# Mamba scan with a mixture-of-experts branch: halo columns through a side buffer, and other slot tables

## Chip, cores and metric

One NeuronCore of one Trainium2 chip. The metric is the device time of one execution in microseconds (us), lower is better; the time before is the median of three executions.

## What is computed

`x` is (2, 2048, 256). It is normalised over its last axis (`xn`), and the output is `x + mamba(xn) + moe(xn)`. Cut to what matters:

```python
x_in, z = split(xn @ W_in)                       # 512 channels each
u = silu(causal_conv4(x_in) + conv_b)            # 4 taps along the time axis
dt, B, C = split(u @ W_xproj)                    # 16 + 16 + 16
delta = softplus(dt @ W_dt + b_dt)
h_t = exp(delta_t * A) * h_{t-1} + delta_t * u_t * B_t    # 16 states per channel
y_t = sum_n h_t[n] * C_t[n];   mamba = ((y + D_skip * u) * silu(z)) @ W_out
# moe: router softmax, top 2 of 16 experts, each: W1 -> layernorm -> exact gelu -> W2
```

## The kernel before

The 4096 rows are cut into 8 chunks (`NC`) of 512 time steps (`T`), four chunks to a sequence (`CPB`). In a chunk there are 4 channel blocks (`DC`) times 16 states (`NS`) = 64 **units**, numbered g = 0 to 511 over the kernel; a unit's number inside its chunk is its **slot**. The work of one unit:

- ScalarE (ACT), `exp_unit(g)`: `hb = exp(delta * A)`, into a ring of 12 rows (`HR`). ACT issues it six units (`LEAD`) ahead of its own slot, and it waits until the product of unit g-12 with C has read the ring row.
- VectorE (DVE): `product(g)` makes `psB = B * du`, `scan(g)` runs the recurrence over 512 steps in place in `hb`.
- The product with C is made for two units at once, by GpSimd (POOL) in `unit_pair(g)`; the pairs listed in `HC_DVE` are made by DVE in `times_c(g)` instead, right behind the pair's second scan. Either waits on `s_tr >= g + 2 - GR` (`GR` = 6): TensorE must have summed unit g-5, since the result goes into a ring of six rows.
- TensorE (PE), `sum_unit(g)`: four transposing matmuls add the product into `psY`, four units (`LAG`) behind PE's own slot.

Every engine walks through the 512 slots in program order, and nothing synchronises the slots of two engines but the semaphores. All other work is hung into slots by the tables `AT` (chunks 1 to 6), `AT0` (chunk 0), `AT7` (chunk 7) and, for the 20 expert groups that start at the units `GS`, `MOE` (offsets from the start). The names that matter here:

- `x_mm`, `x_in`, `x_copy`, `x_silu`: for the next chunk, project a channel block (2 matmuls), copy it from PSUM into a row of the ring `ux` (6 rows of 3 halo columns and 512 steps), convolve it (4 matmuls of the shifted row), copy back, silu. Each waits for the one before. In `x_in` ACT copies the block, and then copies its last three columns straight from PSUM into the halo columns of the row that the chunk after will use.
- `xd_mm`, `xd_copy`, `d_mm`, `d_exp`, `d_ln`, `d_max`: the projection to dt, B and C, and softplus, which ends in DVE's `d_max` (L1377). All of it goes through the one bank `psA`, so `x_mm` of the next chunk waits for the fourth `d_max` of the present one.
- `du` (POOL), `du_copy` (DVE): delta times u; `dskip` (PE): the D_skip term, first into `psY`.
- `z_mm`, `z_copy`, `z_silu`, `gate`: the gate branch. `gate(c, dc)` (DVE, L1571) waits until PE has summed the 16 units of its channel block. `gate`'s fourth entry is run in the chunk after.
- `e_tr`, `e_mm`, `e_trc`, `e_copy`: output projection of the chunk before, through bank `psC`.
- `MOE`: `load`/`load1`/`load2` are SP's loads, `t1` transposes rows on PE, `t1c` copies them on ACT (L845), `w1`, `hn`, `t2`, `t2c`, `gelu`, `w2`, `yo`, `put` follow. Banks `psC` are taken in turns (`C_TURN`), in the order in which ACT evicts them.

On DVE, slots are taken two by two: two products, two scans, then `times_c`, then all `d_max` and `gate` work of both slots. Moving an entry from slot 4 to 5, or from 3 to 2, leaves DVE's order as it was; moving one from 37 to 38 puts it one pair later. In one slot PE does `dskip`, then `sum_unit`, then the rest.

The last state of each unit is carried over a chunk boundary by ACT's `carries` (slot given by `carry`, modulo 4). Routing (16 zero rows and 64 row scatters by POOL's indirect DMAs) ends in the first 90 units.

Of the kernel before, what the change touches and what calls it, by code (L numbers as in the profile page):

```python
# [42 lines left out]
INIT_AT = 58  # L43
ETAB_AT = 40
# [35 lines left out]
    "x_load": [33],  # L80
    "x_mm": [7, 8, 10, 11, 12, 13, 18, 21, 22, 22, 23, 23, 27, 32, 32, 32, 32, 34, 34, 34, 35, 35, 37, 37],
    "x_in": [10, 19, 30, 34],
    "x_copy": [12, 22, 32],
# [18 lines left out]
AT7 = {
    "d_mm": [37, 45, 47, 3],
    "d_exp": [42, 52, 59, 4],
    "d_ln": [34, 35, 52, 6],
    "d_max": [46, 56, 61, 7],
    "du": [62, 9, 20, 36],
    "z_mm": [9, 19, 24, 29],
    "z_copy": [15, 24, 26],
    "z_silu": [32],  # L110
    "gate": [37, 42, 55, 3],
    "dskip": [0, 11, 34, 44],
    "carry": [0],
    "p_tr": [53, 56, 59, 61],
    "p_trc": [56, 58, 59, 62],
    "p_mm": [56, 58, 59, 61],
    "p_copy": [58, 58, 61, 62],
}
# [1516 lines left out]
```

## Time and profile before

| | us |
|---|---|
| three executions | 1137.55, 1130.39, 1132.38 |
| median | 1132.38 |
| the profiled execution | 1137.55 |
| its span, first to last instruction | 1135.8 |
| first scan starts | 70.1 |
| last scan ends | 1119.3 |

So the eight chunks take 1049.2 us of the span; what lies ahead is normalisation, routing and the first chunk's input, and what lies behind is the last output projection. A row of the timeline reads: start, length, engine, line, operation, output<-input, shape, count, and in brackets the idle time before it with what ended it. Merged rows overlap by some hundredths, since an instruction is started before the one ahead has drained.

### The profile page before, as it was taken

The page shows a single profiled execution, that of the slowest core. Times are in us where ns is not written, and L with a number is a line of the kernel's source. Part 1 is how long each engine was busy: PE and PEld are TensorE (multiplying, and loading weights), DVE is VectorE, ACT ScalarE, POOL GpSimd, SP SyncE. Part 2 cuts the span into 40 slices and gives each one's busy share as a digit, 9 for nine tenths or more (in the row PEclk, how much of TensorE's full clock was granted, in tenths as well). Part 3 has the DMA queues.
Part 4 walks back from the last instruction along what each step waited for, and adds up shares of the span by engine and source line. Part 5 has one row for each costly group of instructions (what it writes and reads, how often), then busy time and mean ns, then how long its engine had stood idle before and what let it go on. Part 6 is the DMA issues. An engine that isn't in the chain of part 4 may idle for free.

```text
span 1135.8 us, 16904 instructions
## 1 busy us (share of the span) xinstructions
PE 940.2 (83%) x4570; PEld 639.2 (56%) x4571; DVE 1045.8 (92%) x1308; ACT 864.9 (76%) x1839; POOL 871.0 (77%) x562
## 2 busy tenths in 40 slices
PE   4927776497998999779998999899988999887865
PEld 3414343363566656556666766576656666666544
DVE  7887999999999988968998989999999999999894
ACT  4544698556698799857999689978998799976971
POOL 5057899699778788756878767977987887887894
PEclk9957887589889999879997999899997999889989
DMA  9576457973376424825447652873457543855313
GB/s 305 188 271 241 137 183 225 316 291 83 112 245 204 107 69 122 312 82 112 103 104 233 210 107 67 255 235 57 107 151 249 133 116 87 291 169 108 70 19 65
DMA packets 119367, 185.86 MB, mean 164 GB/s; under 512 B 12012, under 2 KB 104344, under 8 KB 111016
## 3 DMA queue, kind: packets, MB, share of 16 engines
q1 hardware_dynamic: 87120, 144.60, 37.7%
q0 software_dynamic: 19584, 25.26, 13.0%
q10 hardware_dynamic: 12568, 14.93, 4.3%
q8 instruction: 36, 0.59, 0.2%
q14 instruction: 59, 0.48, 0.1%
HBM read 146.34 MB, written 42.60 MB: 166 GB/s over the span
## 4 chain that ended last, share of the span: by engine, by line
PE 36%; DVE 18%; issue 16%; ACT 14%; POOL 9%; DMA 4%; ACTq 2%; SPq 1%; POOLq 0%; DVEq 0%
DVE hb L1555 10%; PE psY L1087 8%; POOL hc L624 5%; PE psA L1112 4%; PE psC L1225 4%; PE psA L1160 3%; ACT hb L798 3%; PE psE L1202 3%; PE psC L1175 3%; PE psA L1104 2%; DVE psB L1544 2%; ACT hnT L913 2%; PE psA L1148 2%; DMA xg<-xs_d 1%; POOL xs_d L638 1%
## 5 line engine op out<-in xcount | busy, mean ns | idle before, releaser
L624 POOL TENSOR_TENSOR hc<-hb,Cb 128x1024 f32<-128x1024 f32 x245 | 621.2, 2640 | 108.2 <-PE psY L1087 65.4
L1555 DVE TENSOR_TENSOR_SCAN hb<-hb,carry,psB 128x512 f32<-128x512 f32 x384 | 470.9, 1261 | 6.8 <-ACT hb L798 5.0
L798 ACT ACTIVATE hb<-delta,aneg 128x512 f32<-128x512 f32 x512 | 351.9, 716 | 27.5 <-POOL hc L624 21.0
L1087 PE MATMUL psY<-ident,hc 128*128 128x128 f32 x2048 | 308.0, 292 | 71.1 <-POOL hc L624 70.8
L1087 PEld LDWEIGHTS psY<-ident,hc 128*128 128x128 f32 x2048 | 258.1, 151 | 183.8 <-POOL hc L624 94.1
L1544 DVE TENSOR_TENSOR psB<-Bb,psU 128x512 f32<-128x512 f32 x512 | 324.6, 678 | 3.2 <-DMA Bb<-bc_d 3.2
L672 POOL DMA_INDIRECT out<-yo,idx x80 | 128.8, 1610 | 56.8 <-DMA out<-yo,idx 16.9
L1555 DVE TENSOR_TENSOR_SCAN hb<-hb,psB 128x512 f32<-128x512 f32 x128 | 149.3, 1202 | 0.0
L1112 PE MATMUL psA<-ux,dgw 128*128 128x512 f32 x232 | 114.0, 607 | 1.6 <-ACT ux L739 1.4
L1225 PE MATMUL psC<-w2r,hnT 128*128 128x256 f32 x320 | 89.8, 429 | 0.0
L631 POOL TENSOR_TENSOR du<-delta,ux 128x512 f32<-128x512 f32 x32 | 47.2, 1474 | 53.9 <-DVE delta L1377 51.8
L1202 PE MATMUL psE<-w1r,xgT 128*128 128x256 f32 x320 | 85.0, 411 | 0.0
L1225 PEld LDWEIGHTS psC<-w2r,hnT 128*128 128x128 f32 x320 | 63.9, 210 | 18.8 <-issue 10.4
L1202 PEld LDWEIGHTS psE<-w1r,xgT 128*128 128x128 f32 x320 | 60.9, 200 | 17.5 <-issue 10.1
L1104 PE MATMUL psA<-xnT,win 128*128 128x512 f32 x116 | 59.2, 629 | 11.7 <-ACT zs L822 7.8
L1160 PE MATMUL psA<-win,xnT 128*128 128x512 f32 x128 | 63.8, 623 | 1.1 <-ACT ux L745 1.1
L913 ACT ACTIVATE hnT<-hnT,vecs 128x128 f32<-128x128 f32 x160 | 63.8, 480 | 0.3
L1175 PE MATMUL psC<-wout,ygT 128*128 128x256 f32 x248 | 61.0, 389 | 1.3 <-ACT ygT L831 1.2
L1148 PE MATMUL psA<-xr,rows 16*128 16x512 f32 x60 | 42.0, 786 | 20.3 <-DVE delta L1377 19.6
L1112 PEld LDWEIGHTS psA<-ux,dgw 128*128 128x128 f32 x232 | 40.9, 196 | 27.3 <-issue 23.4
L1175 PEld LDWEIGHTS psC<-wout,ygT 128*128 128x128 f32 x248 | 45.9, 196 | 7.4 <-ACT ygT L831 2.0
L638 POOL DMA_INDIRECT xs_d<-xg,slots x37 | 39.2, 1059 | 14.2 <-issue 7.0
(233 smaller groups left out, 1198.2 us busy)
## 6 DMA issues: line engine op xcount, KB each, us to landing
Bb<-bc_d SPq DMA_DIRECT2D x32, 1024.0 KB, 7.1
Cb<-bc_d SPq DMA_DIRECT2D x32, 1024.0 KB, 7.4
w1r<-w1c_d SPq DMA_DIRECT2D x80, 256.0 KB
w2r<-in_L_ffn_W SPq DMA_DIRECT2D x80, 256.0 KB, 3.4
xg<-xs_d SPq DMA_DIRECT2D x20, 516.0 KB
xg<-xn_d SPq DMA_DIRECT2D x37, 128.0 KB, 2.8
Bb<-in_L_attn_x SPq DMA_DIRECT2D x8, 512.0 KB, 8.2
xn_d<-hb SPq DMA_DIRECT2D x8, 512.0 KB, 7.9
```

What stands on the lines that cost most here:

```text
L624: pool.tensor_tensor(hc[:, k:k + 2, :], hb[:, g % HR:g % HR + 2, :], Cb[:, n:n + 2, :], ALU.mult).then_inc(s_g, 1)
L672: pool.indirect_dma_start(out=out[:, :], out_offset=bass.IndirectOffsetOnAxis(ap=idx[:, g % 2, j:j + 1], axis=0), in_=yo[:, j, :], in_offs ...
L798: act.activation(hb[:, g % HR, :], delta[:, dc, :], ACT.Exp, scale=aneg[:, dc, n:n + 1]).then_inc(s_exp, 1)
L913: ins = act.activation(hnT[:, j, kc, :], hnT[:, j, kc, :], ACT.Gelu, scale=g1t[:, bass.ds(e, 1), kc], bias=be1t[:, bass.ds(e, 1), kc])
L1087: mm = pe.matmul(y[:, tt * P:(tt + 1) * P], hc[:, g % GR, tt * P:(tt + 1) * P], ident[:, :], start=False, stop=(n == NS - 1), is_transpose ...
L1112: mm = pe.matmul(bank[:, :], dgw[:, dc, k, :], x_of(p, dc)[:, k:k + T], start=(k == 0), stop=(k == KW - 1))
L1160: mm = pe.matmul(psA[:, :], xnT[:, c % 2, kc, tt * P:(tt + 1) * P], win[:, 1, kc, :], start=(kc == 0), stop=(kc == KC - 1))
L1175: mm = pe.matmul(psC[:, 0:D], ygT[:, dc, :], wout[:, dc, :], start=(dc == 0), stop=(dc == dc_out(c) - 1))
L1202: mm = pe.matmul(psE[:, a * D:(a + 1) * D], xgT[:, a, kc, :], w1r[:, a, kc, :], start=False, stop=(kc == KC - 1), skip_group_check=True)
L1225: mm = pe.matmul(psC[:, a * D:(a + 1) * D], hnT[:, 2 * h + a, kc, :], w2r[:, 2 * h + a, kc, :], start=False, stop=(kc == KC - 1), skip_gro ...
L1544: dve.tensor_tensor(psB[g % 2][:, :], Bb[:, n, :], psU[:, :], ALU.mult).then_inc(s_dbu, 1)
L1555: dve.tensor_tensor_scan(h, h, psB[g % 2][:, :], first, ALU.mult, ALU.add).then_inc(s_scan, 1)
```

## The change

The halo of a channel block no longer goes from PSUM into the row of the next chunk. `x_in` now makes three copies, in this order: the row's own halo columns (from zeros at the start of a sequence, else from a new side buffer `halo` that the chunk before filled), the last three columns of the PSUM bank into `halo`, and the block itself. All three count on `s_xi`, which the convolution waits for. With that, a `memset` of `ux` on DVE and PE's wait for DVE's constants at its start are gone. The last chunk makes the three copies too, where it made one.

The other part is in the tables. One `HC_DVE` list takes the place of another: pairs 180, 204, 274 and 416 go to POOL, pairs 22, 64, 72, 78 and 142 come to DVE. `AT`, `AT0`, `AT7`, `MOE`, `CEN0`, `INIT_AT` and `ETAB_AT` have entries moved by one to seven slots.

```diff
-INIT_AT = 58
-ETAB_AT = 40
+INIT_AT = 53
+ETAB_AT = 42
...
 AT = {
-    "x_load": [36],
+    "x_load": [33],
-    "xd_copy": [46],
-    "d_mm": [50, 55, 58, 3],
+    "xd_copy": [47],
+    "d_mm": [50, 55, 57, 3],
-    "d_max": [55, 58, 62, 4],
-    "du": [53, 0, 25, 26],
+    "d_max": [55, 58, 62, 5],
+    "du": [53, 4, 24, 29],
-    "gate": [30, 45, 54, 3],
+    "gate": [30, 45, 52, 2],
...
 AT0 = {
-    "d_mm": [46, 50, 59, 6],
+    "d_mm": [47, 51, 59, 4],
...
-    "d_max": [50, 58, 62, 18],
-    "d0_exp": [4, 6, 6],
-    "d0_max": [7, 8, 8],
+    "d_max": [51, 59, 60, 15],
+    "d0_exp": [2, 3, 5],
+    "d0_max": [5, 7, 9],
...
-    "gate": [33, 41, 52, 27],
+    "gate": [31, 43, 50, 25],
...
-    "carry": [1],
+    "carry": [0],
...
 AT7 = {
-    "z_silu": [32],
-    "gate": [37, 42, 55, 3],
+    "z_silu": [33],
+    "gate": [38, 41, 55, 3],
...
-HC_DVE = [2, 10, 12, 20, 54, 56, 86, 180, 204, 274, 416]
+HC_DVE = [2, 10, 12, 20, 22, 54, 56, 64, 72, 78, 86, 142]
...
 MOE = {
-    "load": [0],
-    "load1": [0, 3],
+    "load": [1],
+    "load1": [1, 4],
-    "t1": [2, 13],
+    "t1": [3, 13],
-    "idx": [6],
+    "idx": [9],
-    "t2c": [14, 22],
+    "t2c": [13, 22],
...
-CEN0 = 19
+CEN0 = 21
...
+        halo = sb("halo", [P, 2, DC, HALO])
...
                 act.wait_ge(s_du, j - UR + 1)
+                if p == 0:
+                    act.wait_ge(s_cdve, NCONST)
+                elif p % CPB:
+                    act.wait_ge(s_xi, 3 * (j - DC) + 2)
+                act.activation(x_of(p, dc)[:, 0:HALO], halo0[:, :] if p % CPB == 0 else halo[:, (p - 1) % 2, dc, :], ACT.Copy).then_inc(s_xi, 1)
+                act.activation(halo[:, p % 2, dc, :], bank[:, T - HALO:T], ACT.Copy).then_inc(s_xi, 1)
                 act.activation(u_of(p, dc), bank[:, :], ACT.Copy).then_inc(s_xi, 1)
-                if p + 1 < NC:
-                    if j + DC >= UR:
-                        act.wait_ge(s_xp, j + DC - UR + 1)
-                    if p == 0:
-                        act.wait_ge(s_cdve, NCONST)
-                    act.activation(x_of(p + 1, dc)[:, 0:HALO], halo0[:, :] if (p + 1) % CPB == 0 else bank[:, T - HALO:T],
-                                   ACT.Copy).then_inc(s_xi, 1)
...
-                    pe.wait_ge(s_xi, 2 * (p * DC + dc + 1) if p + 1 < NC else 2 * p * DC + dc + 1)
+                    pe.wait_ge(s_xi, 3 * (p * DC + dc + 1))
...
             pe.wait_ge(s_const, 2)
-            pe.wait_ge(s_cdve, NCONST)
...
-            dve.memset(ux[:, 0:DC, 0:HALO], 0.0).then_inc(s_cdve, 1)
```

## Rows read from the trace of the kernel before

**Rows 1.** The page's first two parts: busy time, and TensorE's granted clock.

```profile
PE 940.2 (83%) x4570; PEld 639.2 (56%) x4571; DVE 1045.8 (92%) x1308; ACT 864.9 (76%) x1839; POOL 871.0 (77%) x562
...
PEclk9957887589889999879997999899997999889989
```

**Rows 2.** Busy time in windows, slots 1 to 45 of chunks 1, 3, 5, then clock, DMA.

```profile
233.50:321.30 87.80, 76.18 (x351) 48.30 (x350) 87.77 (x100) 56.98 (x122) 75.14 (x47) 0.94 0.48 149
...
489.10:587.40 98.30, 91.15 (x426) 60.52 (x425) 84.52 (x98) 77.97 (x151) 67.88 (x45) 0.96 0.35 80
...
754.20:842.10 87.90, 85.51 (x420) 57.52 (x419) 86.47 (x101) 76.99 (x161) 72.56 (x44) 1.00 0.47 117
```

**Rows 3.** Groups of instructions by shape: DVE's pairs, POOL's pairs, the halo copy.

```profile
L624 POOL TENSOR_TENSOR hc<-hb,Cb 128x1024 f32<-128x1024 f32 x245 | 621.2, 2640 | 108.2 <-PE psY L1087 65.4 <-DVE hb L1555 39.7 <-ACT yo L926 1.3
...
L1564 DVE TENSOR_TENSOR hc<-hb,Cb 128x1024 f32<-128x1024 f32 x11 | 20.0, 1821 | 22.6 <-PE psY L1087 22.4
...
L739 ACT ACTIVATE ux<-psA 128x3 f32<-128x3 f32 x21 | 3.6, 170 | 0.0
```

**Rows 4.** DVE's timeline at the four pairs that leave it: 180, 204, 274, 416.

```profile
454.17 1.23 DVE L1564 TENSOR_TENSOR hc<-hb,Cb 128x1024 f32<-128x1024 f32 x1 [3.57 <-PE psY L1087]
...
515.99 1.22 DVE L1564 TENSOR_TENSOR hc<-hb,Cb 128x1024 f32<-128x1024 f32 x1 [12.74 <-PE psY L1087]
...
658.31 1.22 DVE L1564 TENSOR_TENSOR hc<-hb,Cb 128x1024 f32<-128x1024 f32 x1 [3.89 <-PE psY L1087]
...
933.25 3.14 DVE L1564 TENSOR_TENSOR hc<-hb,Cb 128x1024 f32<-128x1024 f32 x1
```

**Rows 5.** ACT's and DVE's timelines at unit 228, at unit 302, at unit 430.

```profile
556.58 1.94 ACT L798 ACTIVATE hb<-delta,aneg 128x512 f32<-128x512 f32 x3
...
559.00 1.26 DVE L1544 TENSOR_TENSOR psB<-Bb,psU 128x512 f32<-128x512 f32 x2
560.17 2.44 DVE L1555 TENSOR_TENSOR_SCAN hb<-hb,carry,psB 128x512 f32<-128x512 f32 x2
562.53 1.27 DVE L1544 TENSOR_TENSOR psB<-Bb,psU 128x512 f32<-128x512 f32 x2
...
706.55 0.72 ACT L798 ACTIVATE hb<-delta,aneg 128x512 f32<-128x512 f32 x1
...
707.91 1.21 DVE L1555 TENSOR_TENSOR_SCAN hb<-hb,psB 128x512 f32<-128x512 f32 x1
...
956.50 0.72 ACT L798 ACTIVATE hb<-delta,aneg 128x512 f32<-128x512 f32 x1
957.11 0.20 ACT L804 ACTIVATE carry<-hb 128x4 f32<-128x4 f32 x1
957.21 1.94 ACT L798 ACTIVATE hb<-delta,aneg 128x512 f32<-128x512 f32 x3
...
959.34 1.28 DVE L1555 TENSOR_TENSOR_SCAN hb<-hb,carry,psB 128x512 f32<-128x512 f32 x1
```

**Rows 6.** Timelines in chunk 0's first units: DVE's fourth d_max; PE; ACT.

```profile
96.37 0.75 DVE L1377 SCALAR_TENSOR_TENSOR delta<-psA,vecs,tmpA 128x512 f32<-128x512 f32 x1 [3.51 <-ACT tmpA L787]
...
89.38 2.82 PE L1087 MATMUL psY<-ident,hc 128*128 128x128 f32 x12 [24.78 <-POOL hc L624]
92.13 2.07 PE L1148 MATMUL psA<-xr,rows 16*128 16x512 f32 x2
...
94.23 0.69 ACT L780 ACTIVATE tmpA<-psA,bneg 128x512 f32<-128x512 f32 x1 [2.16 <-PE psA L1148]
```

**Rows 7.** Timelines at chunk 0's slots 50 to 52: PE, then DVE.

```profile
188.75 2.07 PE L1148 MATMUL psA<-xr,rows 16*128 16x512 f32 x2 [2.56 <-DVE delta L1377]
...
193.81 0.69 DVE L1571 TENSOR_TENSOR zs<-zs,psY 128x512 f32<-128x512 f32 x1 [1.67 <-PE psY L1087]
```

**Rows 8.** DVE's timeline at three other stalls: units 66, 150 and 486.

```profile
227.18 0.69 DVE L1571 TENSOR_TENSOR zs<-zs,psY 128x512 f32<-128x512 f32 x1 [2.65 <-PE psY L1087]
...
389.37 2.45 DVE L1555 TENSOR_TENSOR_SCAN hb<-hb,carry,psB 128x512 f32<-128x512 f32 x2 [1.74 <-ACT carry L804]
...
1070.84 0.69 DVE L1571 TENSOR_TENSOR zs<-zs,psY 128x512 f32<-128x512 f32 x1 [2.57 <-ACT zs L822]
```

**Rows 9.** Who waited for whom, whole run: us in total, times, longest us.

```profile
ACT xgT L845 <- PE psC L1184: 2.8, 5, 1.1
```

More of the change, by code:

```diff
@@ L79 @@
 AT0 = {
[L80 to L83, printed above, removed]
+    "x_load": [26],
+    "x_mm": [7, 7, 10, 11, 12, 13, 18, 21, 22, 22, 23, 23, 27, 32, 32, 32, 32, 33, 34, 34, 35, 35, 36, 36],
+    "x_in": [9, 19, 30, 34],
+    "x_copy": [13, 22, 32],
     "x_silu": [38],
-    "xd_mm": [37, 41, 43, 43],
+    "xd_mm": [38, 41, 43, 45],
     "xd_copy": [43],
-    "d_mm": [46, 50, 59, 6],
-    "d_exp": [47, 52, 59, 7],
-    "d_ln": [48, 54, 59, 9],
-    "d_max": [50, 58, 62, 18],
-    "d0_exp": [4, 6, 6],
-    "d0_max": [7, 8, 8],
-    "du": [50, 8, 21, 35],
-    "z_mm": [14, 18, 23, 26],
-    "z_copy": [17, 19, 23],
+    "d_mm": [47, 51, 59, 4],
+    "d_exp": [45, 52, 58, 5],
+    "d_ln": [49, 55, 60, 10],
+    "d_max": [51, 59, 60, 15],
+    "d0_exp": [2, 3, 5],
+    "d0_max": [5, 7, 9],
+    "du": [50, 4, 21, 30],
+    "z_mm": [14, 18, 23, 27],
+    "z_copy": [16, 18, 22],
     "z_silu": [26],
-    "gate": [33, 41, 52, 27],
-    "dskip": [3, 13, 35, 51],
-    "bc_load": [47, 57, 63, 63],
-    "carry": [1],
+    "gate": [31, 43, 50, 25],
+    "dskip": [3, 9, 36, 51],
+    "bc_load": [47, 57, 62, 62],
+    "carry": [0],
 }
 AT7 = {
[L103 to L109, printed above, removed]
-    "z_silu": [32],
-    "gate": [37, 42, 55, 3],
[L112 to L115, printed above, removed]
+    "d_mm": [44, 48, 53, 1],
+    "d_exp": [36, 51, 60, 3],
+    "d_ln": [35, 42, 59, 6],
+    "d_max": [47, 57, 62, 6],
+    "du": [62, 9, 19, 34],
+    "z_mm": [11, 21, 24, 30],
+    "z_copy": [15, 24, 27],
+    "z_silu": [33],
+    "gate": [38, 41, 55, 3],
+    "dskip": [4, 9, 35, 40],
+    "carry": [1],
+    "p_tr": [55, 57, 59, 60],
+    "p_trc": [55, 58, 59, 60],
     "p_mm": [56, 58, 59, 61],
-    "p_copy": [58, 58, 61, 62],
+    "p_copy": [57, 58, 60, 62],
 }
-HC_DVE = [2, 10, 12, 20, 54, 56, 86, 180, 204, 274, 416]
+HC_DVE = [2, 10, 12, 20, 22, 54, 56, 64, 72, 78, 86, 142]
 PUT0 = -1
@@ L424, in build @@
         NBIG = 5
-        NCONST = 7
+        NCONST = 6
         xt = x.rearrange("(g a p) d -> g p a d", p=P, a=TT)
```

## Prediction

> **What bounds the kernel now.** I read the page's busy times first. DVE is busy 92% of the span, PE 83%, POOL 77% and ACT 76% [rows 1]. That alone says that DVE is the bound, and that whatever takes work or idle time off DVE shortens the run. The windows by part of a chunk say that this is half the truth. In slots 1 to 45 of chunk 5, PE is busy 85.51 of 87.90 us at a granted clock of 1.00 while DVE is busy 86.47 of the same: both are full. In chunk 1 the same slots have DVE at 87.77 of 87.80 and PE at 76.18: DVE alone binds. In chunk 3, PE is busy 91.15 of 98.30 and DVE only 84.52: PE binds, and DVE's idle time is a symptom [rows 2]. So from chunk 2 on there are two regimes. In slots 5 to 45 PE carries the next chunk's input, the gate branch and the output projection, and ACT is tied to it, since it evicts each of these in order. From slot 46 on PE has little but sums, and DVE binds. In chunks 0 and 1 DVE binds throughout.
>
> The reader is to take one thing from this: an idle DVE microsecond is worth a microsecond only if the exponentials that its later scans read are ready that much earlier than they are used. How much earlier is read in two timelines, by the end of an exponential on ACT and the start of the scan of the same unit on DVE. I call that the slack. It is small around slot 46, right behind ACT's silu of the next chunk, because this silu stands at the end of PE's long chain.
>
> **Pairs that leave DVE.** Each of the four costs its own time and the stall in front of it, where DVE waits for PE's sum of unit g-5 [rows 4].
>
> - 204: 12.74 + 1.22 = 14.0 us of DVE. Chunk 3 is where PE binds. Unit 228's exponential, the first of three from 556.58, ends near 557.3, and its scan starts at 560.17 [rows 5]. If ACT's times stay, DVE can be 2.9 us earlier there and no more. I take 2.9; the other bound is 14.0.
> - 274: 3.89 + 1.22 = 5.1 us. Unit 302's exponential ends at 706.55 + 0.72 = 707.27, its scan starts at 707.91: slack 0.6. I take 0.6; bound 5.1.
> - 416: 3.1 us of its own, no stall. Unit 430: 957.22 against 959.34, slack 2.1. I take 2.1; bound 3.1.
> - 180: 3.57 + 1.23 = 4.8 us. It lies behind slot 46, so DVE binds. But `gate(2, 2)` moves from slot 54 to 52, and then stands right behind the scans of units 180 and 181, waiting for the sum of unit 175, which is the very sum that the pair waited for. The stall stays and has another name. I take 1.2; if PE comes earlier by itself, 4.8.
>
> Sum: 2.9 + 0.6 + 2.1 + 1.2 = 6.8 us gained, against 27.0 if DVE's time were the whole story. For POOL, which is busy 77%, these are four pairs more and five less.
>
> **Pairs that come to DVE.** The eleven of before have a mean of 1.821 us [rows 3], from 1.22 to 3.14 [rows 4]. Pair 22 stands in chunk 0 and pairs 72 and 78 in chunk 1, where nothing hides them: 3 x 1.8 = 5.4 us. Pair 64 stands just ahead of a `gate` that waits 2.65 us for PE, and pair 142 ahead of a stall of 1.74 us on ACT [rows 8]: cover enough, so nothing; without it 3.6 us. They relieve POOL in the part where it scatters the routed rows, but no scan there waits for POOL, so I give nothing for that.
>
> The 3.14 us of pair 416 ran beside a product of POOL's, the 1.22 did not. The Trainium skill (SBUF — State Buffer, section "SBUF: two separate sides") says that DVE and GpSimd share one port pair as an exclusive lock, which a DVE operation with two SBUF inputs takes part in, and that the loser blocks for the whole instruction. The trace agrees as far as it goes. By that rule a DVE pair costs 1.2 us beside an idle POOL and up to POOL's whole instruction more beside a busy one. It gives a rival below.
>
> **First units.** Of `d_max` 1 to 3 in chunk 0, the last waits 3.51 us, because `d_mm(0, 3)` stands in PE's slot 6, behind three sums (12 matmuls, 2.82 us) that begin only when POOL's first pair is ready at 89.38; its ACT work starts at 94.23 and the result is used at 96.37 [rows 6]. In slot 4 the matmul stands behind one sum instead of three, that is 2/3 x 2.82 = 1.9 us earlier, and it runs alone, not as the second of two, 1.0 us earlier by half of 2.07. `d0_exp` 2 and 3 now lie ahead of the exponential that waits for POOL, so ACT is free for it. The wait ahead of the fourth `d_max` and 0.8 us ahead of the third shrink: I take 1.9 + 1.0 + about 0.2 = 3.1 us, bounds 0 and 3.51 + 0.8 = 4.3. Afterwards DVE binds, so it stays gained.
>
> **Gate in chunk 0.** The third `gate` waits 1.67 us for PE, which itself waited 2.56 us in `d_mm(1, 1)` of slot 50 for DVE [rows 7], ahead of the sum of unit 47. The gate moves a pair earlier (559.00 to 562.53, so 3.5 us [rows 5]), which alone would cost 3.5 us more of waiting; but `d_mm` moves to slot 51, behind that sum in PE's order, and PE no longer waits there. I take 1.7 us gained; if the sum isn't ready, up to 1.7 + 3.5 lost against that.
>
> **Last chunk.** The first `gate` waits 2.57 us for ACT's z [rows 8]. It moves one pair later (two products and two scans, 3.5 us), and z one slot later (1.8 us, half a pair): 3.5 - 1.8 = 1.7, of which all is gained: 1.8 us with rounding; bounds 0 and 2.6.
>
> **Halo.** 4 blocks x 7 chunks get one small copy more, and the last chunk's 4 get two: 36. Such a copy takes 0.17 us [rows 3], but ACT starts the next instruction 0.10 us after a small one has started (957.11 and 957.21 [rows 5]), since they overlap. It lies on ACT, ahead of the convolution that PE waits for. Where ACT has no slack at slot 46, four copies cost 0.4 us; that is some chunks of 2 to 6, and elsewhere DVE hides it. I take 1.0 us lost, bounds 0 and 36 x 0.17 = 6.1. The new wait on `s_xi` is for ACT's own copies a chunk ago and holds up nothing; the one on `s_cdve` is for memsets long done, and the exponentials behind it wait for nothing new. The `memset` and PE's first wait go from a place where PE waits for the normalised rows anyway: nothing. Without that cover, one small instruction, about the 0.17 us of the small copy.
>
> **Other moves.** `d_max` 4 to 5, `gate` 3 to 2 and `du` 25 to 24 leave the order as it was. `du` 0 to 4 and 26 to 29 let POOL's pair go first and are still ahead of DVE's copy in slots 14 and 46: nothing. `xd_copy`, `x_load`, `load`, `load1`, `idx`, `CEN0`, `INIT_AT` and `ETAB_AT` move work and DMA issues that have slots to spare, past no wait that is late today; `ETAB_AT` moves DVE work inside a DVE-bound chunk. `t1` 2 to 3 is the one that I don't give away: see the third rival.
>
> **Sum.** -6.8 + 5.4 - 3.1 - 1.7 - 1.8 + 1.0 = -7.0 us. Against the profiled execution, 1137.55, that is 1130.5. This one was 5.2 us above the median of the three runs, 1132.38, so the forecast for the median is 1132.4 - 7.0 = **1125.4 us**, 0.6% faster.
>
> **Rival 1, DVE's time counts in full.** The exponentials come earlier too, because PE and ACT are not really full. For it: the Trainium skill (Perfetto Trace Analysis, section "Identifying the Most-Contended Engine") warns that the busy share of matmuls says little of how close TensorE is to its limit, and wants the busy share of weight loads, which in chunk 5's window is 57.52 of 87.90. By that page there would be a third left. Against it: PE's matmuls follow each other there without gaps, 85.51 of 87.90, and fewer microseconds need fewer or faster matmuls, which the change doesn't bring. Time: the gains for 204, 274 and 416 become 14.0, 5.1 and 3.1, so 16.6 more: 1125.4 - 16.6 = 1108.8 us.
>
> **Rival 2, nothing is left.** The new DVE pairs meet POOL, which is at its busiest in chunks 0 and 1 (75.14 of 87.80 in chunk 1's window [rows 2]), and each costs 3.1 us as pair 416 did. Pairs 22, 72, 78 cost 9.3 in place of 5.4, pairs 64 and 142 outgrow their cover by 0.5 + 1.4 = 1.9, and the halo copies cost 2.8 in place of 1.0: 7.6 more, 1133.0 us. Pair by pair it depends on where POOL stands, so I don't expect all five.
>
> **Rival 3, slower.** `t1` on PE moves from offset 2 to 3, its copy on ACT stays at 4. Where PE and ACT run level, ACT gets to the copy before PE has made the transposes, and the exponentials behind it in ACT's queue wait, and DVE's scans for them. Today this wait is 2.8 us over 5 of 40 copies [rows 9]. A PE slot is about 87.9 / 44 = 2.0 us; half a slot for each of the 20 groups is 20 us, so 1125.4 + 20 = 1145.4. It makes the run slower than before from 7.0 / 20 = 0.35 us a group, and by over 1% from 0.9. Against it: 14 of the 20 groups start outside slots 28 to 45, where there is slack of several us.
>
> **How the numbers follow.** Forecast 0.45, rival 1 0.18, rival 2 0.22, rival 3 0.15. The forecast's own range is 1118 to 1131: the bounds of the halo and of the gates on one side, half of pair 204 on the other. Over 1% faster means under 1121.1; a change of less than about 1% can hardly be told from none. All of rival 1 and 0.19 of the rest lie there: 0.37. Over 1% slower (above 1143.7) is two thirds of rival 3: 0.10. Within 1%: 0.53. The range for 8 in 10 is 1111 to 1140, which leaves out the far part of rivals 1 and 3.
>
> **What would show it.** Right: in slots 1 to 45 of chunk 3 PE is as busy as before and DVE's idle time is spread over waits for `hb`; chunk 1 is longer by 3 to 4 us; the fourth `d_max` of chunk 0 comes near 93.3; at slot 52 of chunk 2 the `gate` waits some 3.5 us for PE; the gaps of `times_c` fall from 22.6 to some 2 us. Wrong: chunk 3's window of 98.30 us falls to near chunk 5's 87.90 (rival 1); DVE pairs of 3 us (rival 2); ACT's copy L845 idle before it by 10 us or more (rival 3). The clock could undo all of it: chunk 3 starts at a low granted clock, and whether it does so again depends on when PE falls idle at the chunk's end, which I can't forecast.

## The result, and the profile after

| us | before | after |
|---|---|---|
| median (executions) | 1131.28 (7) | 1140.44 (7) |
| lowest to highest | 1126.86 to 1137.55 | 1135.98 to 1144.74 |
| the profiled execution | 1137.55 | 1138.76 |
| its span | 1135.8 | 1137.0 |

The ratio is 1.0076, with a 95% interval of 1.0048 to 1.0104: the change costs some 9 us, where 7 us less were forecast. Of 40 executions of after, 39 lie between 1133.56 and 1148.23 us, with a median of 1139.34, and one, at a mean granted clock of 0.554, took 1550.57 and is in none of the other figures. The two profiled executions differ by 1.2 us only, since that of before was one of its longest and that of after lies under its own median. A cause can therefore not be read from one pair of traces; it took kernels with one part of the change each (next section).

The busy times of after, the page's first part, then TensorE's granted clock [rows 1]:

```profile
PE 935.7 (82%) x4571; PEld 639.7 (56%) x4571; DVE 1044.7 (92%) x1308; ACT 866.9 (76%) x1875; POOL 867.4 (76%) x561
...
PEclk9967895697979999889998999899997999899887
```

PE is busy 4.5 us less than before, POOL 3.6 and DVE 1.1 us less, ACT 2.0 us more. So in these two traces no engine has more work that would pay for 9 us; what the change costs is waiting. The windows answer to [rows 2], again from the sum of slot 1 to the same sum as there, in chunks 1, 3 and 5 of after:

```profile
228.60:316.60 88.00, 77.17 (x347) 48.86 (x346) 87.90 (x101) 57.68 (x126) 69.20 (x45) 0.91 0.46 141
486.80:583.80 97.00, 89.69 (x427) 59.78 (x425) 84.57 (x98) 78.33 (x155) 69.91 (x43) 0.98 0.36 82
755.70:845.10 89.40, 85.23 (x419) 57.54 (x418) 87.55 (x102) 77.51 (x165) 73.06 (x48) 1.00 0.48 123
```

Chunk 3 went from 98.30 to 97.00 us, nowhere near chunk 5's length, and chunk 5 from 87.90 to 89.40. Chunk 1, which the new pairs 72 and 78 were to lengthen by 3 to 4 us, went from 87.80 to 88.00: they took 1.22 and 1.23 us, and pair 86 in the same window took 1.51 us where it had 3.27 before (the last section says why). The groups of after, by shape: DVE's pairs, POOL's pairs, the two halo copies, and the matmuls of `d_mm`, the last row of all being that of before, which was not shown ahead (busy us, mean ns | idle before, and what ended it):

```profile
L1562 DVE TENSOR_TENSOR hc<-hb,Cb 128x1024 f32<-128x1024 f32 x12 | 20.1, 1676 | 1.6 <-PE psY L1087 1.3
L625 POOL TENSOR_TENSOR hc<-hb,Cb 128x1024 f32<-128x1024 f32 x244 | 616.6, 2667 | 113.7 <-PE psY L1087 73.8 <-DVE hb L1553 29.9 <-ACT yo L926 4.6
L738 ACT ACTIVATE ux<-halo 128x3 f32<-128x3 f32 x32 | 6.4, 201 | 10.8 <-PE psA L1104 8.1 <-PE psC L1104 1.0 <-PE psY L1104 1.0
L739 ACT ACTIVATE halo<-psA 128x3 f32<-128x3 f32 x29 | 4.6, 160 | 0.0
L1148 PE MATMUL psA<-xr,rows 16*128 16x512 f32 x60 | 41.7, 781 | 34.8 <-DVE delta L1375 34.1 <-ACT xr L765 0.7
```

```profile
L1148 PE MATMUL psA<-xr,rows 16*128 16x512 f32 x60 | 42.0, 786 | 20.3 <-DVE delta L1377 19.6 <-ACT xr L765 0.7
```

The gaps of DVE's pairs fell from 22.6 to 1.6 us, as wanted [rows 3]. What has grown is the wait of `d_mm` for `d_max`, from 19.6 to 34.1 us.

### The profile page after: what moved, and what is told of

It is laid out like the page before. It is cut to its first block, busy times and chain, and to the rows that moved or that the text cites. A ratio compares the mean times of both kernels' runs of the same rounds, so it can differ in the third digit from the quotient of the medians.

```text
span 1137.0 us, 16966 instructions
## 1 busy us (share of the span) xinstructions
PE 935.7 (82%) x4571; PEld 639.7 (56%) x4571; DVE 1044.7 (92%) x1308; ACT 866.9 (76%) x1875; POOL 867.4 (76%) x561
## 4 chain that ended last, share of the span: by engine, by line
PE 39%; ACT 18%; issue 15%; DVE 12%; POOL 10%; ACTq 3%; DMA 2%; SPq 0%; POOLq 0%; DVEq 0%
PE psY L1087 9%; POOL hc L625 7%; DVE hb L1553 6%; ACT hb L798 5%; PE psC L1225 5%; PE psA L1112 4%; PE psC L1175 4%; PE psE L1202 3%; PE psA L1160 3%; PE psA L1104 3%; ACT hnT L913 3%; PE psA L1148 2%; POOL out L673 2%; DVE psB L1542 1%; DMA xg<-xs_d 1%
## 5 line engine op out<-in xcount | busy, mean ns | idle before, releaser
L1225 PE MATMUL psC<-w2r,hnT 128*128 128x256 f32 x320 | 89.7, 429 | 0.0
L1225 PEld LDWEIGHTS psC<-w2r,hnT 128*128 128x128 f32 x320 | 63.8, 210 | 18.5 <-issue 10.2
L1148 PE MATMUL psA<-xr,rows 16*128 16x512 f32 x60 | 41.7, 781 | 34.8 <-DVE delta L1375 34.1
L1160 PE MATMUL psA<-win,xnT 128*128 128x512 f32 x128 | 61.2, 601 | 1.5 <-ACT ux L745 1.1
L926 ACT ACTIVATE yo<-psC,wv 128x256 f32<-128x256 f32 x80 | 33.3, 469 | 27.2 <-PE psC L1225 24.2
```

Source lines behind the costliest of these rows:

```text
L1160: mm = pe.matmul(psA[:, :], xnT[:, c % 2, kc, tt * P:(tt + 1) * P], win[:, 1, kc, :], start=(kc == 0), stop=(kc == KC - 1))
L1225: mm = pe.matmul(psC[:, a * D:(a + 1) * D], hnT[:, 2 * h + a, kc, :], w2r[:, 2 * h + a, kc, :], start=False, stop=(kc == KC - 1), skip_gro ...
```

## Experiments

Each kernel is the one before with the stated edit, unless it says otherwise. Its ratio to the kernel before is from executions on the same chip, so medians of different rows are not to be compared with each other. n is the number of executions.

| kernel | edit | median (n) | ratio | 95% interval |
|---|---|---|---|---|
| list_only | all of `HC_DVE` | 1131.31 (12) | 0.9979 | 0.9959 to 0.9998 |
| list_drop | 180, 204, 274, 416 to POOL, none added | 1128.31 (12) | 0.9988 | 0.9972 to 1.0003 |
| halo_only | the halo through the side buffer | 1131.99 (12) | 0.9998 | 0.9977 to 1.0019 |
| tables_only | all of `AT`, `AT0`, `AT7`, `INIT_AT`, `ETAB_AT`, `CEN0` | 1137.82 (12) | 1.0034 | 1.0013 to 1.0056 |
| at_only | `AT` | 1136.06 (12) | 1.0030 | 1.0009 to 1.0052 |
| at0_only | `AT0`, the three constants | 1130.50 (12) | 1.0001 | 0.9980 to 1.0022 |
| at7_only | `AT7` | 1131.03 (12) | 0.9986 | 0.9969 to 1.0002 |
| moe_only | all of `MOE` | 1139.13 (6) | 1.0070 | 1.0043 to 1.0098 |
| moe_loads | `load`, `load1`, `idx` | 1138.21 (6) | 1.0070 | 1.0050 to 1.0090 |
| moe_t1 | `t1` | 1135.03 (12) | 1.0039 | 1.0020 to 1.0057 |
| moe_t2c | `t2c` | 1131.79 (12) | 1.0006 | 0.9988 to 1.0023 |
| moe_load01 | `load`, `load1` | 1132.12 (12) | 1.0016 | 0.9992 to 1.0039 |
| moe_idx | `idx` | 1137.21 (12) | 1.0060 | 1.0035 to 1.0085 |
| fill9 | four extra copies on POOL at offset 9 | 1131.41 (12) | 1.0004 | 0.9980 to 1.0027 |
| fill6 | the same at offset 6 | 1131.16 (12) | 1.0003 | 0.9984 to 1.0021 |
| after_old_moe | after, with `MOE` of before | 1137.56 (6) | 1.0053 | 1.0032 to 1.0073 |
| after_idx6 | after, with `idx` back at 6 | 1135.61 (12) | 1.0034 | 1.0016 to 1.0052 |
| best | `HC_DVE` and `AT7` | 1131.23 (12) | 0.9995 | 0.9977 to 1.0013 |

### The four parts of the change

list_only, halo_only, tables_only and moe_only each take over one part of the diff, whole. The theory was that the pairs bring back less than their slack, the rivals that a table or the halo costs.

> The kernel before with the new HC_DVE list alone. Slack theory (a DVE microsecond counts only up to the slack of the exponentials): 6.8 us gained and 5.4 us lost, so -1.4 us, ratio 0.999. Theory that DVE time counts in full: -27.0 + 5.4 = -21.6 us, ratio 0.981. Theory that the list is what made the changed kernel slower (the pairs in chunks 0 and 1 cost 3 us each or more, and POOL falls behind where it took pairs over): +5 to +10 us, ratio 1.004 to 1.009.

> The kernel before with the halo's way through the side buffer alone, all tables as before. My prediction: +1.0 us, ratio 1.001. Theory that the order of the three copies makes it slower (two small copies stand ahead of the block's own copy, so each convolution starts later, on PE's full stretch): 28 blocks times 0.2 to 0.3 us, +5.6 to +8.4 us, ratio 1.005 to 1.0075.

> The kernel before with the new AT, AT0 and AT7 and the moved constants INIT_AT, ETAB_AT, CEN0 alone, the list, MOE and the halo as before. My prediction: -3.1 -1.7 -1.8 us = -6.6 us, ratio 0.994. Rival: the gates and softplus steps moved earlier wait for what is not ready, +3 us or more, ratio 1.003 or more.

> The kernel before with the new MOE offsets alone. My prediction: 0, ratio 1.000. Third rival (the row transposes one slot later on PE, ACT waits for them ahead of its copy and the exponentials behind it are late): +5 to +20 us, ratio 1.005 to 1.018.

The list gains 0.2%, the halo is worth nothing either way, and the two parts that were costed at next to nothing cost 0.3% and 0.7%. Added up this is +0.81%, against +0.76% for the whole: the four parts account for it.

### Inside the expert table

```diff
 moe_t1:       -    "t1": [2, 13],       +    "t1": [3, 13],
 moe_t2c:      -    "t2c": [14, 22],     +    "t2c": [13, 22],
 moe_load01:   -    "load": [0], "load1": [0, 3],    +    "load": [1], "load1": [1, 4],
 moe_idx:      -    "idx": [6],          +    "idx": [9],
 moe_loads:    both of moe_load01 and moe_idx
```

> The kernel before with the first row transposes (t1) in offset 3 in place of 2, nothing else. Theory T1 (these transposes a slot later on PE are what the MOE offsets cost, since the two slots between them and the first products with W1 shrink to one and ACT's copy lies in between): most of the 0.70% of moe_only, ratio 1.004 to 1.007. Theories T2 and L below: 1.000.

> The kernel before with ACT's copy of the first half's second transposes (t2c) in offset 13 in place of 14. Theory T2 (ACT gets to the copy before PE has made the transposes, and exponentials wait behind it): ratio 1.003 to 1.007. T1 and L: 1.000.

> The kernel before with load in offset 1, load1 in 1 and 4, and idx in 9 (before: 0, 0 and 3, 6). Theory L (SP loads the routed rows later behind loads of B and C, or POOL makes the row numbers later): ratio 1.003 to 1.007. T1 and T2: 1.000.

> The kernel before with load in offset 1 and load1 in 1 and 4 (before 0, and 0 and 3), nothing else. Theory S (the routed rows and W1 are asked for behind what SP waits for in the slot between, so they land later; the groups that start at slots 56 and 57 of a chunk fall behind a load of B and C): ratio 1.004 to 1.007. Theory I: 1.000.

> The kernel before with idx (POOL's row numbers of an expert group) in offset 9 in place of 6, nothing else. Theory I (POOL is disturbed by the four small operations in their new place): ratio 1.004 to 1.007, most of the 0.70% of moe_loads. Theory S (it is SP's loads): 1.000.

`idx` alone costs 0.6%: four short instructions on POOL, three slots later. What it does is seen in the second half of chunk 4. POOL's timeline of moe_load01, where `idx` is at offset 6:

```profile
694.00 2.94 POOL L624 TENSOR_TENSOR hc<-hb,Cb 128x1024 f32<-128x1024 f32 x1
696.34 0.90 POOL L656 TENSOR_SCALAR padv<-xg,padrow 128x4 f32<-128x4 f32 x1
696.62 0.75 POOL L657 COPY wv<-xg 128x4 f32<-128x4 f32 x1
697.46 0.20 POOL L659 TENSOR_TENSOR padv<-xg,padv 128x4 f32<-128x4 f32 x1
697.72 0.19 POOL L661 CAST idx<-padv 128x4 int32<-128x4 f32 x1
702.97 2.36 POOL L624 TENSOR_TENSOR hc<-hb,Cb 128x1024 f32<-128x1024 f32 x1 [5.06 <-DVE hb L1555]
705.48 1.63 POOL L672 DMA_INDIRECT out<-yo,idx  x1 [0.15 <-issue]
706.61 2.90 POOL L624 TENSOR_TENSOR hc<-hb,Cb 128x1024 f32<-128x1024 f32 x1
709.79 1.59 POOL L672 DMA_INDIRECT out<-yo,idx  x1 [0.28 <-DMA out<-yo,idx]
```

The same of moe_idx, then its PE and its DVE:

```profile
703.05 2.37 POOL L624 TENSOR_TENSOR hc<-hb,Cb 128x1024 f32<-128x1024 f32 x1 [5.81 <-PE psY L1087]
705.58 1.58 POOL L672 DMA_INDIRECT out<-yo,idx  x1 [0.15 <-issue]
706.60 2.95 POOL L624 TENSOR_TENSOR hc<-hb,Cb 128x1024 f32<-128x1024 f32 x1
708.93 0.91 POOL L656 TENSOR_SCALAR padv<-xg,padrow 128x4 f32<-128x4 f32 x1
...
711.05 1.62 POOL L672 DMA_INDIRECT out<-yo,idx  x1 [0.54 <-PE psY L1087]
712.16 5.23 POOL L624 TENSOR_TENSOR hc<-hb,Cb 128x1024 f32<-128x1024 f32 x2
...
715.13 0.66 PE L1087 MATMUL psY<-ident,hc 128*128 128x128 f32 x4 [1.34 <-POOL hc L624]
...
723.54 0.75 DVE L1377 SCALAR_TENSOR_TENSOR delta<-psA,vecs,tmpA 128x512 f32<-128x512 f32 x1 [1.05 <-ACT tmpA L787]
```

At offset 6 the four instructions lie in a gap of POOL's that costs nothing. At offset 9 they stand between a pair and a row add in a stretch without gaps: both kernels start a pair within 0.01 us of each other (706.61 and 706.60), and the pairs after it start at 710.82 and 712.16, 1.34 us apart. PE's next sum waits the same 1.34 us, and DVE's `d_max` 1.05 us. The place decides, not the work, which is the same 1.6 us in both.

The other groups agree. In before, POOL stands idle for over 1 us right behind the four instructions in 14 of the 20 groups, 49.2 us in all; in moe_idx in 2 of 20, 8.8 us in all. Another measure is the end of each unit's scan on DVE, set against the end of the same scan in another trace. By it moe_idx loses 3.9 us on moe_load01 from unit 80 to the last. Its median is 6.7 us above before's; the trace shows less, since its profiled execution (1133.74) is 3.5 us under that median.

fill9 and fill6 ask whether POOL's time at those offsets costs by itself. They add copies that nothing reads:

```diff
+                            if off == 9:      # 6 in fill6
+                                for k in range(4):
+                                    pool.tensor_copy(fil[:, k, :], zrow[:, 0:GT])
```

> The kernel before, idx in offset 6 as it was, with four extra small POOL copies (128 x 4, zeros into a spare tile, nothing waits for them) in offset 9 of each of the 20 groups. Capacity theory (from offset 8 on POOL has a row add in nearly every pair of units, so any POOL work there delays the pairs that PE sums): about as much as moe_idx or a little more, ratio 1.004 to 1.008. Theory that idx costs through what waits for its result or through the work it waits for: 1.000 to 1.001.

> The same four extra copies in offset 6, right behind idx. Capacity theory: POOL has slack there, ratio 1.000 to 1.002. Theory that POOL is at its limit everywhere and about 1 us of POOL work costs the same in any slot: the same as fill9, 1.004 or more.

Neither costs anything that can be measured. In the group rows the 80 copies of fill9 are busy for 15.9 us, that is 0.8 us a group, those of fill6 for 10.9; the four instructions of `idx` take from 696.34 to 697.91, 1.57 us. If the cost went with POOL's time at offset 9, fill9 would cost 0.8 / 1.57 of 0.60%, which is 0.31%; its interval ends at 0.27%. But `idx`'s own interval, 0.35 to 0.85%, makes that 0.18 to 0.43%, so this doesn't hold the two apart. Excluded is a cost of 0.4% or more for 0.8 us of POOL's time at offset 9, as the capacity theory had it. Whether `idx` costs more than its time on POOL, by its chain of semaphore waits or by what waits for its result, stays open.

`t1` costs 0.39%. Rival 3 named a place for it: ACT's copy L845 waiting for PE. That wait, over the whole run, in moe_t1 and then in after (us, times, longest) [rows 9]:

```profile
ACT xgT L845 <- PE psC L1184: 3.6, 5, 1.1
...
ACT xgT L845 <- PE psC L1184: 7.0, 6, 1.9
```

In moe_t1 it is 0.8 us more than in before. So the mechanism is there, and the wait that shows isn't the price: 0.39% is 4.4 us (2.3 to 6.4), against 0.8 us of wait. The largest loss against halo_only's trace is 2.7 us at the start of chunk 4, where the last `gate` of chunk 3 waits 3.44 us for PE (0.77 in halo_only); but before's own profiled execution waits 3.71 us there. And moe_t1's profiled execution (1131.41) is 3.6 us under its median, so most of the cost may not be in this trace at all. What `t1` costs, and by what, is not settled.

### Inside the slot tables

```diff
 at_only, its core:
-    "d_mm": [50, 55, 58, 3],     "gate": [30, 45, 54, 3],
+    "d_mm": [50, 55, 57, 3],     "gate": [30, 45, 52, 2],
 at0_only, its core:
-    "d_max": [50, 58, 62, 18],   "d0_exp": [4, 6, 6],
+    "d_max": [51, 59, 60, 15],   "d0_exp": [2, 3, 5],
 at7_only, its core:
-    "z_silu": [32],              "gate": [37, 42, 55, 3],
+    "z_silu": [33],              "gate": [38, 41, 55, 3],
```

> The kernel before with the new AT alone (chunks 1 to 6: x_load, xd_copy 47, third d_mm 57, du 4, 24, 29, third gate 52). I predicted nothing for it beside the gate. Theory A (gate in slot 52 waits 3 to 4 us for PE in each of chunks 2 to 4, and xd_copy a slot later delays the softplus chain at the chunk's end): ratio 1.002 to 1.005. Theory B (AT7): 1.000.

> The kernel before with the new AT0 (chunk 0) and INIT_AT, ETAB_AT, CEN0 alone. My prediction: -3.1 -1.7 = -4.8 us, ratio 0.996. The trace of tables_only shows 3.2 us lost by the start of chunk 1 against the profiled execution before; if that is the tables' whole cost, ratio 1.003.

> The kernel before with the new AT7 (chunk 7) alone. My prediction: -1.8 us, ratio 0.998. Theory B (the later z matmuls and the earlier softplus of the last block cost at the start and middle of chunk 7): ratio 1.002 to 1.004.

`AT` is the one that costs. By the ends of its scans it falls behind halo_only mostly at the seams between chunks: by 1.9 us from unit 112 to 128, 0.6 from 176 to 192, 3.8 from 240 to 272, 0.8 from 304 to 320, 0.9 from 368 to 384. Of the 3.8, 2.7 aren't `AT`'s to pay: they are the wait of the last `gate` of chunk 3 for PE, 3.43 us here and 3.71 in before, where halo_only has 0.77. Chunk 7, which `AT` doesn't touch, differs by another 2.9. The seam at slot 57 of chunk 1 in at_only, PE's, ACT's and DVE's timelines:

```profile
330.82 1.09 PE L1087 MATMUL psY<-ident,hc 128*128 128x128 f32 x8
336.04 2.07 PE L1148 MATMUL psA<-xr,rows 16*128 16x512 f32 x2 [4.13 <-DVE delta L1377]
...
339.62 3.78 PE L1225 MATMUL psC<-w2r,hnT 128*128 128x256 f32 x8
...
343.44 0.84 ACT L926 ACTIVATE yo<-psC,wv 128x256 f32<-128x256 f32 x2 [3.14 <-PE psC L1225]
...
345.44 0.75 DVE L1377 SCALAR_TENSOR_TENSOR delta<-psA,vecs,tmpA 128x512 f32<-128x512 f32 x1 [1.77 <-ACT tmpA L787]
```

and in before, PE and DVE:

```profile
338.49 1.12 PE L1148 MATMUL psA<-xr,rows 16*128 16x512 f32 x2
...
344.94 0.72 DVE L1377 SCALAR_TENSOR_TENSOR delta<-psA,vecs,tmpA 128x512 f32<-128x512 f32 x1
```

The edit is `d_mm` 58 to 57 for the third channel block. This matmul writes `psA`, which the second `d_max` frees at DVE's slot 58. In before PE did a sum and the second half of an expert product first, and the bank was free by then. One slot earlier, PE stands for 4.13 us with this matmul at the head of its queue. All that follows is late: an expert output, for which ACT waits 3.14 us, then the softplus behind it, then DVE, 1.77 us. On top of it, the two matmuls of `d_mm` take 2.07 us after PE's idle time and the eight of L1225 3.78, where before has 1.12 and 2.27. The granted clock behind PE's busy times shows why; the first row is of at_only, the second of before:

```profile
333.14:343.38 10.24, 7.34 (x16) 4.24 (x17) 10.24 (x12) 7.03 (x18) 6.21 (x3) 0.50 0.92 314
```

```profile
330.06:336.88 6.82, 6.82 (x19) 3.81 (x18) 6.82 (x9) 6.14 (x13) 6.30 (x8) 0.50 0.86 297
```

Both fall to the lower level (1.2 GHz), before for 6.82 us, at_only for 10.24 from a moment inside the wait. After shows the same at the same place: 4.84 us of PE's wait, 1.77 us of DVE's. Over the whole run, `d_mm` waits for `d_max` 35.3 us in at_only, 21.1 in halo_only. No kernel has the one `d_mm` entry alone, so what `xd_copy`, the `du` entries and the third `gate` add to the 0.30% is not known.

`AT0` wins 1.15 us at the third `gate` of chunk 0 (0.52 us of wait against 1.67) and gives it back behind: its third `d_max`, moved from slot 62 to 60, waits 2.13 us where before has no wait, and the two waits after it are 1.28 and 1.94 us against 2.65 and 1.41, so 1.3 us more in all. At the first units it gains nothing either: the fourth `d_max` comes 24.56 us behind the first scan's start, 26.26 in before, but pair 10 behind it takes 3.96 us and not 2.42, and at unit 12 DVE is where it was. `AT7` gains 0.14%, within its interval of nothing.

### The list without its additions

```diff
-HC_DVE = [2, 10, 12, 20, 54, 56, 86, 180, 204, 274, 416]
+HC_DVE = [2, 10, 12, 20, 54, 56, 86]
```

> The kernel before with pairs 180, 204, 274 and 416 given to POOL and none given to DVE. Slack theory: 2.9 + 0.6 + 2.1 + up to 4.8 for pair 180, whose gate stays in slot 54 here, so -6.8 to -10.4 us, ratio 0.991 to 0.994. Theory that DVE time counts in full: -27.0 us, ratio 0.976. Theory that POOL is too late with four pairs more: 1.000 or more.

It gains 0.12%, about 1.4 us, where the sum had 6.8 for these four pairs. DVE's stalls in chunk 3 of list_drop, between 500 and 590 us, which are all the rows with idle time there:

```profile
508.33 1.28 DVE L1555 TENSOR_TENSOR_SCAN hb<-hb,carry,psB 128x512 f32<-128x512 f32 x1 [3.34 <-ACT hb L798]
511.02 1.28 DVE L1555 TENSOR_TENSOR_SCAN hb<-hb,carry,psB 128x512 f32<-128x512 f32 x1 [0.22 <-ACT hb L798]
512.51 1.28 DVE L1555 TENSOR_TENSOR_SCAN hb<-hb,carry,psB 128x512 f32<-128x512 f32 x1 [0.21 <-ACT hb L798]
516.68 1.28 DVE L1555 TENSOR_TENSOR_SCAN hb<-hb,carry,psB 128x512 f32<-128x512 f32 x1 [0.52 <-ACT hb L798]
521.70 2.45 DVE L1555 TENSOR_TENSOR_SCAN hb<-hb,carry,psB 128x512 f32<-128x512 f32 x2 [2.55 <-ACT hb L798]
537.70 0.69 DVE L1533 COPY psU<-du 128x512 f32<-128x512 f32 x1 [0.57 <-POOL du L631]
546.14 0.69 DVE L1571 TENSOR_TENSOR zs<-zs,psY 128x512 f32<-128x512 f32 x1 [6.57 <-ACT zs L820]
```

Together 3.34 + 0.22 + 0.21 + 0.52 + 2.55 + 0.57 + 6.57 = 13.98 us. The 12.74 us in front of pair 204 and its own 1.22 were 13.96. Before has 1.04 us of waiting for the same `gate`, so 12.9 us came back in these rows, within 40 us of time and under three other names. The rest went too: by the ends of its scans list_drop is 5.10 us ahead of before at unit 204, 18.74 at unit 206 and 5.15 at unit 224. (After and best keep 2.0 and 2.3 us of it there, list_only nothing.) The largest single wait is one that the slack didn't look at: the `gate` at slot 30 waits for ACT's z. ACT had no idle time from 534 us to this z. Before that, from 498 to 534 us, it waited for PE 13 times, 14.1 us in all, and each of these waits is within 0.02 us of the one in before: PE and ACT ran as they had, whatever DVE did.

The same reading for the other three: pair 180 leaves 1.4 us, of which half is gone at unit 198, pair 274 nothing and pair 416 1.1 us, where this kernel's sum had up to 4.8, 0.6 and 2.1.

### Do the parts add up?

```diff
 after_idx6, against after:
-    "idx": [9],
+    "idx": [6],
 best, against before (and AT7 as in at7_only):
-HC_DVE = [2, 10, 12, 20, 54, 56, 86, 180, 204, 274, 416]
+HC_DVE = [2, 10, 12, 20, 22, 54, 56, 64, 72, 78, 86, 142]
```

> The changed kernel with the MOE offsets of before. If the parts add up (list 0.9979, halo 0.9998, tables 1.0034): ratio to the kernel before 1.001, that is 1133 to 1134 us, 6 to 7 us under the changed kernel. If the MOE offsets cost only in the company of the old tables: 1.005 or more.

> The changed kernel with one entry put back: idx at offset 6 instead of 9. Theory (idx alone costs 0.6%, because POOL's four short instructions fall into a stretch where pairs and row adds follow each other without a gap): 1140.4 - 6.8 = 1133.6 us, ratio to the kernel before 1.002 (1.000 to 1.004), that is the AT part (0.3%) and t1 (0.4%) stay, the list (-0.2%) and AT7 (-0.1%) are against them. Rival (in the changed kernel the costs of idx, t1 and AT overlap, each filling slack that another has used, as the kernel with the old MOE table at 1.0053 hints): it stays at 1.005 or above, and the single costs are not a sum.

> The kernel before with only the two parts of the change that measured below 1: the new HC_DVE list (0.9979) and AT7 (0.9986). Theory: they lie in different chunks (1 to 6, and 7), so they add: ratio 0.9965, about 1127.4 us against a before of 1131.4. Rival (DVE's time won ahead of chunk 7 is given back there, since chunk 7 waits for its DMA load and for PE): 0.998 to 1.000.

The four parts do, 0.81% against 0.76%. Smaller pieces come out lower than their sums, each time by about as much as the intervals are wide. Undoing `idx` in the changed kernel takes the ratio from 1.0076 to 1.0034, 0.42% where it costs 0.60% alone; that is inside the theory's range, and the rival's 1.005 is not reached. With all of the old `MOE` it is 1.0053, where 0.9979 x 0.9998 x 1.0034 gives 1.0011: 0.42% apart, with some 0.41% of uncertainty. Inside `MOE`, the four singles sum to 1.21% against 0.70% for the table, 0.51% apart with 0.51% of uncertainty. The two gaining parts together, which should have given 0.9965, give 0.9995, 0.30% apart with 0.31%. (These uncertainties are estimates: the half widths of the intervals, squared, added and rooted.) None of the kernels is faster than before by an amount that this measurement holds apart from none, except the list, barely. That costs share a slack, so that what one edit has used the next can't use again, would explain the pattern; it is argued here, not shown.

## Why the prediction was wrong

The step that failed is the paragraph "Other moves". It costed `idx`, `AT`'s third `d_mm` (not even named there) and the slots of `AT0`'s `d_max` at nothing, by "slots to spare, past no wait that is late today". Against that stand +0.60% for `idx`, 6.8 us, and +0.30% for `AT`, 3.4 us. What the runs show in place of slots to spare: behind `idx` at offset 6 POOL has a gap in 14 of 20 groups, at offset 9 in 2; and `d_mm` a slot earlier comes ahead of the `d_max` that frees its bank, 4.13 us of wait at one seam. The second step that failed is a size, that of the pairs that leave DVE: 1.4 us for 6.8. Point by point:

- **Two regimes, PE and DVE.** Right: chunk 3's window stayed at 97.00 us with DVE's idle time spread over other waits. By rival 1 list_drop would have gained 27.0 us; it gained 1.4. The Trainium skill (Perfetto Trace Analysis, section "Identifying the Most-Contended Engine") wants the busy share of weight loads, beside the share of peak arithmetic, read in place of the busy share of matmuls. Here the trace sides with matmuls, 85.51 of 87.90 [rows 2]: the third that weight loads seem to leave was not there for this change to use.
- **Pairs that leave DVE, 6.8 us.** The mechanism was right, the size too big: 1.4 us (interval -0.3 to 3.2). The slack to the exponential of one later unit was taken, unit 228 for pair 204; that exponential is one of several ends of PE's chain, and a nearer one, the z of the `gate` at unit 222, decided. In list_only and list_drop, DVE's lead over halo_only shrinks across chunk 3 (unit 192 to 224: 3.6 to 2.0 us and 4.9 to 4.3): nothing is won there.
- **The gate at slot 52 of chunk 2** waits 4.15 us for PE, forecast "some 3.5": right. The stall kept its size and changed its name.
- **Pairs that come, 5.4 us.** The rows of after for 22, 72 and 78 are 1.22, 1.22 and 1.23 us, 3.7 in all. Pair 64 took 3.45 us, more than its cover of 2.65. Pair 142 took 1.49, and its cover, the stall of 1.74 us, is gone from after. Rival 2's 3.1 us held for one of five. As list_only (0.9979) and list_drop (0.9988) don't differ, the five together cost nothing that shows; 5.4 us, 0.48%, is outside the uncertainty of that difference, about 0.25%. (The mean of 1.8 us hid two kinds of pair, see the last section; and the longest of the eleven was pair 86 with 3.27, not 416 with 3.14.)
- **First units, 3.1 us.** Wrong, and hidden by luck. DVE is 3.3 us earlier at unit 12 in after, which looks like a hit. But the wait ahead of the fourth `d_max` was to shrink and is 3.46 us, against 3.51; the `d_max` comes at 94.70, not near 93.3. After's and at0_only's DVE, and before's pair 10:

```profile
79.56 1.29 DVE L1542 TENSOR_TENSOR psB<-Bb,psU 128x512 f32<-128x512 f32 x2 [2.41 <-DMA Bb<-bc_d]
...
94.70 0.75 DVE L1375 SCALAR_TENSOR_TENSOR delta<-psA,vecs,tmpA 128x512 f32<-128x512 f32 x1 [3.46 <-ACT tmpA L787]
...
100.14 1.23 DVE L1562 TENSOR_TENSOR hc<-hb,Cb 128x1024 f32<-128x1024 f32 x1 [1.25 <-PE psY L1087]
```

```profile
101.27 3.96 DVE L1564 TENSOR_TENSOR hc<-hb,Cb 128x1024 f32<-128x1024 f32 x1 [1.87 <-PE psY L1087]
```

```profile
102.26 2.42 DVE L1564 TENSOR_TENSOR hc<-hb,Cb 128x1024 f32<-128x1024 f32 x1 [1.70 <-PE psY L1087]
```

  Of the 3.3 us, 0.7 come from a load of B that DVE waited 2.41 and not 3.16 us for, about 1.0 from the third `d_max`, whose wait of 0.82 us is gone, and 1.6 from pair 10 and the wait ahead of it. With the same `AT0`, at0_only has none of it left at unit 12. "Afterwards DVE binds, so it stays gained" was wrong as well: of the 3.3 us 2.9 are left at unit 64 and 1.0 at unit 128, and at0_only measures 1.0001.
- **Gate in chunk 0, 1.7 us.** Its wait fell from 1.67 to 0.64 us, so 1.0; the third `d_max`, which stood nowhere in the sum, now waits 2.14 us.
- **Last chunk, 1.8 us.** The working gives 3.5 - 1.8 = 1.7. at7_only measures 1.6 us, with none at all inside its interval; the wait of 2.57 us is gone from its trace.
- **Halo, 1.0 us lost.** Measured 0.2 us gained, interval 2.6 gained to 2.2 lost. Nothing contradicts it, and it wasn't needed.
- **Rival 3.** Right side, right edit, wrong row. It gave `t1` 20 us by half a slot for each of 20 groups; the measured cost is 4.4 us, and the wait that it named is 0.8 us of it in the trace.

The forecast's base was sound: 5.2 us were taken off for the profiled execution, and before's median over 7 to 35 executions is 1130 to 1133 us. The change lost 9 us where the forecast gained 7, and the time, 1140.44, lies 0.4 us above the range. The range's upper end came out of rival 3 alone; the terms costed at nothing had been given no bounds. Nor does the forecast's own upper end, 1131, follow from the bounds named for it: the halo's 5.1 us alone reach 1130.5, and the 5.2 us of the gate in chunk 0 come on top.

## What to carry to other kernels

In a kernel where two or three engines are nearly full in turns, cost each moved slot by asking what stands at the head of that engine's queue at the new place, and look for the gap that covered it at the old one: here 1.6 us of work in a gap were free, and cost 1.3 us in a stretch that had none. Be wary of issuing an instruction a slot earlier when it waits for another engine's late slot; the 4.13 us that it stood there were passed on to what stood behind it, 3.14 us to ACT and 1.77 to DVE. Idle time of the second-busiest engine is worth no more than the slack to the nearest of all the places where it meets the busier one's chain, and the gains and losses of single edits, each under 0.5%, should be measured together before their sum is believed. A forecast that comes out at the right place is worth a look at the rows that it was made of: the 3.3 us at unit 12 were made of others.
